# Feed-forward chunks for both images at once, the 64-channel remainders on halves of TensorE's array, and a new order of all pieces

## The chip, the cores and the metric

The kernel runs on one core of a Trainium2 chip. The metric is the device time in microseconds of one execution. A core has TensorE (PE, matrix products into PSUM), VectorE (DVE), ScalarE (ACT), GpSimd (POOL) and SyncE (SP, which here only issues DMAs). Each engine works through its own instructions in order; semaphores tie the engines together.

## The reference, cut to what matters

```python
h = tokenize(x)                       # 64 images, 196 patches of 768 values, layernorm, W: 768 -> 192, + positions
h = concatenate([h, txt], axis=1)     # 196 + 128 = 324 tokens of 192 channels per image
h = h + attn(layernorm(h))            # selective scan: h_t = exp(delta*A)*h + delta*B*x, y = sum over 16 states of h*C
h = h + ffn(layernorm(h))
# ffn: routed part: sigmoid gate over 128 experts, top 6, each expert silu(x@Wg)*(x@Wu)@Wd with hidden size 464
#      shared part: silu(x @ Wsg) * (x @ Wsu) @ Wsd with hidden size 928, for every token
```

All is float32. The change touches the shared part of `ffn`, and the order of everything that runs beside it.

## The kernel before

`build` runs two phases. `phase1` handles the images two at a time (32 pairs): embedding, first layernorm, the scan over 16 states, second layernorm, the gate and the choice of experts, and the shared feed-forward part. `phase2` goes through the 128 experts and adds their results to the output rows by indirect DMA. The change touches `phase1`, and of the preparation before it two memsets.

A tensor with 192 channels lies as three slabs of 324 columns: slab 0 holds channels 0 to 127 of image 0, slab 1 the same of image 1, and slab 2 holds the 64 remaining channels of both images, image 0 on partitions 0 to 63 and image 1 on partitions 64 to 127. A scan over one state is thus one instruction of 128 x 972.

**Pieces.** Phase 1 is software-pipelined. Its work for one pair is cut into pieces (`scan`, `up_g`, `down`, ...), each with a lag: body i of the loop runs a piece of lag 2 for pair i-2. `schedule` gives every piece a place between 0 and 32 for each engine it uses; the pieces sorted by place are the order of that engine's instructions, the same in every body. The places of different engines are tied to each other only by the semaphores. What sets the order is therefore this list, written out by hand: `scan` n at 2n, and the other pieces around it.

**The scan.** For state n: SP loads `b_wide` (piece `fill_b`, line 437) and `c_wide` (`load_c`, line 443), both broadcasts of a DRAM row to 128 partitions, each by two DMAs of 64 partitions; POOL multiplies `du` by `b_wide` into `state` (line 498); ACT writes the decay into PSUM (`decay`, lines 530 and 531); DVE scans (line 628) and multiplies by `c_wide` (`fill_c`, line 633); POOL adds into `y` (line 508). `b_wide`, `c_wide` and the decay are double-buffered, `state` has four buffers. Before that `bc_values` puts the rows in DRAM, `load_s` fetches one row from there, and `step_size` and `softplus` (ACT, lines 590 to 597, DVE, lines 703 to 705) make `delta` and `du`; line 705 is the last DVE instruction of it, once for each pair.

**The shared feed-forward.** The 928 hidden values are 8 chunks of 116. For chunk and image, 16 in all (k = 2 * chunk + image): `up_g` on PE is two matmuls (line 780 with the 128 channels, line 781 with the slab of remainders, against weights that are zero on the other image's 64 partitions), ACT takes tanh (line 607), DVE makes `ag` (line 765); `up_u` on PE is two matmuls again, and DVE makes `inter` (line 771). The two images use two PSUM banks and two buffers of `th` and `ag`, so one image's chunk can be on PE while the other's is on ACT or DVE. `down_a` and `down` (line 795) multiply `inter` by `ws_d` for each of three row blocks, 8 matmuls for each image and block, and DVE adds them to `h` (line 639).

**Others on PE.** `emb_a` and `emb` (lines 838 and 842): 12 matmuls each for one half image (6 of two columns for the sum of squares, 6 of 194 columns). `resid`, `x1_turn`, `x2_turn`, `gate`, `bc_values`, `count` are short and share one PSUM bank, `work`; `emb` and `down` share another, `sums`. `ln1_apply` and `ln2_apply` are 12 ACT instructions in a row (lines 564 and 565).

Of the kernel before, what the change touches and what calls it, by code (L numbers as in the profile page):

```python
# [9 lines left out]
ALU = mybir.AluOpType  # L10
# [8 lines left out]
PAIRS = B // 2  # L19
# [36 lines left out]

def schedule(engine):
    at = []  # L60

    def put(piece, lag, k, **steps):
        if engine in steps:
            at.append((steps[engine], len(at), (piece, lag, k)))

    for n in range(N):

        b, lag = 2 * n - 4, 0
        if b < 0:
            b, lag = b + 32, -1  # L70
        put("fill_b", lag, n, sp=b, pool=b + 3)
        c, lag = 2 * n - 2.3, 0
        if c < 0:
            c, lag = c + 32, -1
        put("load_c", lag, n, sp=c)
        d, lag = (2 * n - 1.5, 0) if n else (30.5, -1)
        put("decay", lag, n, act=d + 0.3)
        put("scan", 0, n, dve=2 * n)
        put("fill_c", 0, n, dve=2 * n + 1.2, pool=2 * n + 2)
    for k in range(3):  # L80
        put("down_a", 3, k, pe=0.1 + 2 * k)
        put("down", 3, k, pe=1.1 + 2 * k, dve=2.1 + 2 * k)
        put("store_out", 3, k, sp=3.6 + 2 * k)
        put("resid", 1, k, pe=4.9 + 1.8 * k, dve=5.7 + 1.8 * k)
        put("x2_turn", 1, k, pe=15.2 + 1.1 * k, act=16.2 + 1.1 * k)
        put("x1_turn", -1, k, pe=18.2 + 1.1 * k, act=19.2 + 1.1 * k)
    put("load_x", -2, 0, sp=1.5)
    put("load_txt", -1, 0, sp=10.2)
    put("ln2_stats", 1, 0, dve=10.3, act=11.3)
    put("ln2_apply", 1, 0, dve=12.3, act=13)  # L90
    put("emb_scale", -1, 0, dve=11.1)
    put("ln1_stats", -1, 0, dve=12.4, act=13.4)
    put("ln1_apply", -1, 0, dve=14.4, act=15.4)
    for k in range(2):
        put("gate", 1, k, pe=22.1 + k, act=23.3 + k)
        put("emb_a", -2, k, pe=8.5 + 6 * k, act=7.5 + 5.2 * k)
        put("emb", -2, k, pe=9.5 + 5.85 * k, act=13.2 + 5.85 * k)
    put("bc_values", -1, 0, pe=21.5, act=22.3, sp=22.9)
    put("load_s", -1, 0, sp=24.1)
    for k in range(2):  # L100
        put("step_size", -1, k, act=26.2 + k)
    put("softplus", -1, 0, act=28.5, dve=29.2)
    for k in range(3):
        put("choose", 2, k, dve=1.3 + k)
    put("weigh", 2, 0, dve=5)
    put("weigh", 2, 1, dve=6)
    put("count", 2, 0, pe=3.2, dve=5.2)
    put("store_mid", 2, 0, sp=6.5)
    put("find_a", 2, 0, dve=7.5)
    put("find", 2, 0, pe=7.6, dve=8.6)  # L110
    put("emb_stats", -2, 0, dve=20.4, act=21.4)
    for k in range(2 * NJ):
        for n, piece in enumerate(("up_g", "up_u")):
            step = 6.6 + 0.8 * (2 * (k // 2 * 2 + n) + k % 2)
            put(piece, 2, k, pe=step, act=step + 0.6, dve=step + 0.8)
    return [piece for _, _, piece in sorted(at)]
# [7 lines left out]
FIRST_BODY, LOOP_FROM, LOOP_TO, LAST_BODY = -2, 3, 29, PAIRS + 2  # L124
# [7 lines left out]
def bank_uses(i):  # L132

    return [sum(BANK.get(kind) == bank for kind, _, _ in pieces("pe", i)) for bank in (WORK, SUMS)]


def use_number(i, before):


    def use(piece, k, ago=0):  # L140
        bank = BANK[piece]
        same = [(x[0], x[2]) for x in pieces("pe", i - ago) if BANK.get(x[0]) == bank]
        return before[bank] - (len(same) if ago else 0) + same.index((piece, k)) + 1
    return use
# [35 lines left out]
class Buffers:  # L180


    def __init__(self, nc, ctx, ident, found):
# [18 lines left out]
        self.ws_g = sb("ws_g", [128, 3, SHID])  # L202
        self.ws_u = sb("ws_u", [128, 3, SHID])
# [36 lines left out]
def prepare(nc, ctx, a, out, dram_x, b):  # L240
# [4 lines left out]
    with ExitStack() as tmp:  # L245
# [9 lines left out]
        zero_tiles = [b.ident[:], b.ident_bf[:], b.wbc[:], b.wg[:, 1:3], b.ws_g[:, 1:3], b.ws_u[:, 1:3], b.zeros[:],  # L255
# [9 lines left out]
        for half in range(2):  # L265
# [4 lines left out]
                (b.wg[at, 1 + half, :], a["wg_t"][LO:D]), (b.ws_g[at, 1 + half, :], a["ws_g"][LO:D]),  # L270
                (b.ws_u[at, 1 + half, :], a["ws_u"][LO:D]),
# [92 lines left out]
def phase1(nc, ctx, a, out, dram_x, dram_cnt, dram_bc, ident, found):  # L364
# [54 lines left out]
    def bc_rows(t, half, first, rows):  # L419

        at = (2 * t.p + half) * N + first
        return dram_bc[at:at + rows]

    with nc.Block() as block:

        @block.sync
        def _(sp):
            def body(i, todo, use):
                for kind, lag, k in todo:
                    t = i.plus(-lag)  # L430
                    if kind == "fill_b":
# [7 lines left out]
                    elif kind == "load_c":  # L439

                        wait(sp, c_used, N * t.v + k - 1)
                        for half in range(2):
                            sp.dma_start(b.c_wide[k % 2][HI * half:HI * half + HI].rearrange("p a t -> p (a t)"),
                                         bc_rows(t, half, k, 1)[:, 3 * L:6 * L].broadcast_to([HI, 3 * L])).then_inc(c_loaded[k % 2], 16)
                    elif kind == "bc_values":

                        sp.wait_ge(work_free, use(kind, k))
                        wait(sp, c_used, N * (t.v - 1))
                        for image in range(2):
                            rows = b.bcv[N * image:N * image + N]  # L450
                            for half in range(2):
                                to = bc_rows(t, half, 0, N).rearrange("n (c q t) -> n c q t", c=3, q=3)
                                sp.dma_start(to[:, :, image, :], rows).then_inc(bc_stored, 16)
                                if half == image:
                                    sp.dma_start(to[:, :, 2, :], rows).then_inc(bc_stored, 16)
                    elif kind == "load_s":
# [3 lines left out]
                        for half in range(2):  # L460
                            sp.dma_start(b.soft[HI * half:HI * half + HI].rearrange("p a t -> p (a t)"),
# [679 lines left out]
```

## Time and profile before

| | us |
|---|---|
| median of 3 runs (lowest, highest) | 5815.71 (5800.55, 5816.44) |
| the profiled execution, its own time | 5808.81 |
| its span, first to last instruction | 5806.8 |
| PE, DVE busy | 4271.5 (74%), 3764.1 (65%) |
| POOL, ACT busy | 3097.6 (53%), 2051.7 (35%) |
| mean granted TensorE clock | 0.838 |

The span is cut into 40 slices of 145 us in part 2 of the page: phase 1 fills the first 28, phase 2 the rest. Busy shares over the whole span mix the two phases. The granted clock is 1.0 at 2.4 GHz and 0.5 at 1.2 GHz; a share between is a mix of both in time.

### The profile page before, as it was taken

What the parts mean: (1) busy time and instruction counts of PE and PEld (TensorE: products, weight loads), DVE (VectorE), ACT (ScalarE), POOL (GpSimd) and SP (SyncE); (2) the same over time, 40 slices, a digit from 0 to 9 for tenths busy, and PEclk for the clock granted to TensorE, in tenths of its full rate; (3) what the DMA queues carried; (4) which work ended last, traced back from release to release, by engine and by line L of the source; (5) the groups of instructions that cost most, each with busy time, mean ns of one, the idle gap of its engine ahead of it and who ended that gap; (6) DMA issues with size and microseconds to landing.
All of it is one profiled execution on the core that took longest, in us unless ns stands there. A gap on an engine that the chain in (4) does not pass through costs nothing. (4 is left out here: it accounts for less than half of the span.)

```text
span 5806.8 us, 71026 instructions
## 1 busy us (share of the span) xinstructions
PE 4271.5 (74%) x19964; PEld 3364.6 (58%) x19964; DVE 3764.1 (65%) x6446; ACT 2051.7 (35%) x3874; POOL 3097.6 (53%) x1769
## 2 busy tenths in 40 slices
PE   3357777777777777777777777777788788778877
PEld 2335555555555555555555555545677777777777
DVE  2778777778878778777777877786333333333333
ACT  2544454444445444454444445543111111111110
POOL 0765555555556555555555555653255555555554
PEclk7578878888878888878888888889888888888888
DMA  3776666666666666666666666663255555555554
GB/s 89 187 170 172 159 149 156 163 153 166 159 149 161 160 161 157 157 149 156 165 159 157 159 150 161 169 156 90 73 126 126 128 123 128 125 120 128 128 126 105
DMA packets 331418, 837.85 MB, mean 144 GB/s; under 512 B 59152, under 2 KB 143572, under 8 KB 331208
## 3 DMA queue, kind: packets, MB, share of 16 engines
q1 hardware_dynamic: 279928, 764.79, 52.7%
q0 software_dynamic: 49152, 69.84, 6.6%
q10 hardware_dynamic: 2128, 1.26, 0.1%
q14 instruction: 182, 1.49, 0.1%
q8 instruction: 28, 0.46, 0.0%
HBM read 761.92 MB, written 73.75 MB: 144 GB/s over the span
## 5 line engine op out<-in xcount | busy, mean ns | idle before, releaser
L508 POOL TENSOR_TENSOR y<-y,state 128x972 f32<-128x972 f32 x448 | 1027.8, 2294 | 1218.2 <-DVE state L633 1215.3
L498 POOL TENSOR_TENSOR state<-du,b_wide 128x972 f32<-128x972 f32 x512 | 1163.5, 2273 | 356.4 <-DMA b_wide<-bc_rows 191.8
L628 DVE TENSOR_TENSOR_SCAN ps<-ps,state 128x972 f32<-128x972 f32 x512 | 1117.8, 2183 | 106.6 <-POOL state L498 60.6
L780 PE MATMUL ps<-x2f,ws_u 128*116 128x324 f32 x1024 | 503.6, 581 | 574.3 <-DVE ag L765 572.8
L1053 PE MATMUL e_ps<-xgt,w_up 96*116 96x192 f32 x4096 | 730.5, 332 | 24.0 <-DVE e_ag L1026 23.9
L795 PE MATMUL ps<-ws_d,inter 116*98 116x192 f32 (+1 forms) x3072 | 604.9, 360 | 153.4 <-DVE h L639 134.1
L530 ACT ACTIVATE ps<-delta,a_neg 128x648 f32<-128x648 f32 x512 | 410.6, 802 | 855.9 <-DVE state L633 787.3
L1053 PEld LDWEIGHTS e_ps<-xgt,w_up 96*116 96x116 f32 x4096 | 677.3, 183 | 28.4 <-DVE e_ag L1026 26.7
L795 PEld LDWEIGHTS ps<-ws_d,inter 116*98 116x98 f32 (+1 forms) x3072 | 554.8, 193 | 207.6 <-DVE h L639 149.8
L780 PEld LDWEIGHTS ps<-x2f,ws_u 128*116 128x116 f32 x1024 | 190.5, 222 | 763.1 <-DVE ag L765 754.4
L633 DVE TENSOR_TENSOR state<-ps,c_wide 128x972 f32<-128x972 f32 x512 | 596.1, 1164 | 27.0 <-DVE ch L730 9.9
L1011 DVE TENSOR_TENSOR passed<-counts,tk 96x648 f32<-96x648 f32 x128 | 106.2, 829 | 760.9 <-DMA counts<-running_counts,row_idx 760.9
L964 POOL DMA_INDIRECT xg<-token_rows,gather_idx x256 | 244.9, 956 | 647.0 <-DVE gather_idx L1022 592.5
L765 DVE SCALAR_TENSOR_TENSOR ag<-th,ps 116x324 f32<-116x324 f32 x512 | 249.3, 488 | 443.7 <-ACT th L607 441.8
L607 ACT ACTIVATE th<-ps 116x324 f32<-116x324 f32 x512 | 217.2, 434 | 857.1 <-PE ps L781 857.0
L780 PE MATMUL ps<-x2f,ws_g 128*116 128x324 f32 x1024 | 424.2, 499 | 115.7 <-DVE inter L771 111.9
L1088 PE MATMUL e_ps<-w_down,e_inter 116*96 116x192 f32 x2048 | 495.6, 413 | 1.0 <-DVE e_inter L1038 1.0
L781 PE MATMUL ps<-x2f,ws_u 128*116 128x324 f32 x1024 | 455.5, 533 | 0.0
L1088 PEld LDWEIGHTS e_ps<-w_down,e_inter 116*96 116x96 f32 x2048 | 432.0, 217 | 32.7 <-DVE e_inter L1038 1.4
L973 POOL DMA_INDIRECT out_rows<-yo,scatter_idx x256 | 370.7, 1448 | 92.3 <-issue 78.0
L781 PE MATMUL ps<-x2f,ws_g 128*116 128x324 f32 x1024 | 391.7, 466 | 0.0
L842 PE MATMUL ps<-w_tok,x_in 128*98 128x194 f32 x1536 | 389.3, 420 | 0.0
(150 smaller groups left out, 6200.3 us busy)
## 6 DMA issues: line engine op xcount, KB each, us to landing
b_wide<-bc_rows SPq DMA_DIRECT2D x1024, 243.0 KB, 4.9
c_wide<-bc_rows SPq DMA_DIRECT2D x1024, 243.0 KB, 4.1
w_up<-in_we_up SPq DMA_DIRECT2D x128, 696.8 KB
w_down<-in_we_down SPq DMA_DIRECT2D x128, 348.0 KB
x_in<-in_x SPq DMA_DIRECT2D x32, 1176.0 KB, 8.0
soft<-bc_rows SPq DMA_DIRECT2D x64, 243.0 KB, 5.8
bc_rows<-bcv SPq DMA_DIRECT2D x192, 60.8 KB, 2.9
running_counts<-cnt SPq DMA_DIRECT2D x32, 324.0 KB, 3.8
```

Of the source, the lines that this page charges most:

```text
L498: nc.gpsimd.tensor_tensor(b.state[n % 4][:], b.du[t.p][:], b.b_wide[n % 2][:], ALU.mult).then_inc(input_ready, 1)
L508: nc.gpsimd.tensor_tensor(y, y, b.state[n % 4][:], ALU.add).then_inc(y_added, 1)
L530: nc.scalar.activation(to[:, 0:2 * L], b.delta[t.p][:, 0:2, :].rearrange("p a t -> p (a t)"), ACT.Exp, scale=b.a_neg[:, 0, k:k + 1])
L628: nc.vector.tensor_tensor_scan(s, s, b.state[k % 4][:].rearrange("p a t -> p (a t)"), 0.0, ALU.mult, ALU.add).then_inc(scan_done, 1)
L633: nc.vector.tensor_tensor(b.state[k % 4][:].rearrange("p a t -> p (a t)"), state_ps[k % 2], b.c_wide[k % 2][:].rearrange("p a t -> p (a t) ...
L780: nc.tensor.matmul(to, weights[:, 0, cols], b.x2f[t.p][:, q, :], start=True, stop=False)
L781: return nc.tensor.matmul(to, weights[:, 1 + q, cols], b.x2f[t.p][:, 2, :], start=False, stop=True)
L795: mm = nc.tensor.matmul(sums[0:ROWS[k], D * q:D * q + D], b.inter[:, j, q, OFF[k]:OFF[k] + ROWS[k]], b.ws_d[:, j, :], start=(j == 0), stop ...
L842: mm = nc.tensor.matmul(sums[0:98, 196 * c:196 * c + D + 2], b.x_in[:, k, f, at], b.w_tok[:, f, :], start=(f == 0), stop=(f == PC - 1))
L973: nc.gpsimd.indirect_dma_start(out, bass.IndirectOffsetOnAxis(ap=scatter_idx[t.p][:, q:q + 1], axis=0), yo[t.p][:, q, :], None, compute_op ...
L1053: mm = nc.tensor.matmul(ps[0:HC, to_bank + f // 2, CAP * (f % 2):CAP * (f % 2) + CAP], w_up[t.p][:, c, first + HC * f:first + HC * f + HC] ...
L1088: mm = nc.tensor.matmul(ps[0:HALF, 4, D * q:D * q + D], inter[:, f // 2, at:at + HALF], w_down[t.p][:, f, :], start=(f == 0), stop=(f == N ...
```

## The change

1. `up_g` and `up_u` take one chunk for both images: 8 pieces of each instead of 16. On PE a piece is four matmuls (two of 128 channels, two of 64). ACT and DVE get one instruction of 116 x 648 for two of 116 x 324. There is one buffer of `th` and of `ag`, and the two PSUM banks belong to one chunk, so `up_g` k+1 waits for `inter` k.
2. The remainders are multiplied from their own 64 partitions: image 0 with partitions 0 to 63 of weights and data, image 1 with 64 to 127. The zeroed halves of `ws_g` and `ws_u` and their memsets go.
3. `b_wide`, `c_wide` and `soft` are each loaded by one DMA of 128 partitions.
4. `down` and `emb` on PE are cut into four parts each, which can be placed apart (`down`: 4 matmuls each, 12 parts; `emb`: 6 matmuls each, 8 parts). The square of `x_in` on ACT is a piece of its own (`square`).
5. The hand-written places are replaced by a table `PLACES`; a place below 0 or above 32 gives the lag. Every engine's order changes. `load_x` has lag -3, so there is one more body at the start.
6. The count of uses of a PSUM bank is worked out from the order (`use`), with the same meaning.

```diff
+PLACES = {
+    "down": {
+        "pe": (91.23, 92.42, 92.43, 92.56, 94.43, 94.94, 95.9, 96.6, 97.04, 97.16, 97.4, 97.68,),
+        "dve": (102.09, 102.52, 104.48,),
+    },
...
+    "up_g": {
+        "pe": (61.71, 71.04, 73.41, 80.5, 84.48, 86.28, 86.98, 90.7,),
+        "act": (64.27, 70.8, 75.21, 77.26, 83.48, 85.06, 86.85, 92.25,),
+        "dve": (70.31, 75.21, 78.22, 84.67, 86.42, 89.59, 92.67, 96.24,),
+    },
+    "up_u": {
+        "pe": (66.38, 71.56, 79.79, 82.32, 84.85, 86.39, 90.39, 90.99,),
+        "act": (87.43, 98.17, 104.76, 107.65, 109.44, 112.61, 113.55, 125.49,),
+        "dve": (72.94, 76.49, 82.27, 85, 88.16, 91.16, 93.58, 97.56,),
+    },
...
-        self.ws_g = sb("ws_g", [128, 3, SHID])
-        self.ws_u = sb("ws_u", [128, 3, SHID])
+        self.ws_g = sb("ws_g", [128, 2, SHID])
+        self.ws_u = sb("ws_u", [128, 2, SHID])
...
-        zero_tiles = [b.ident[:], b.ident_bf[:], b.wbc[:], b.wg[:, 1:3], b.ws_g[:, 1:3], b.ws_u[:, 1:3], b.zeros[:],
+        zero_tiles = [b.ident[:], b.ident_bf[:], b.wbc[:], b.wg[:, 1:3], b.zeros[:],
...
-                        for half in range(2):
-                            sp.dma_start(b.b_wide[k % 2][HI * half:HI * half + HI].rearrange("p a t -> p (a t)"),
-                                         bc_rows(t, half, k, 1)[:, 0:3 * L].broadcast_to([HI, 3 * L])).then_inc(b_loaded[k % 2], 16)
+                        sp.dma_start(halves(b.b_wide[k % 2]), wide_row(t, k, 0)).then_inc(b_loaded[k % 2], 16)
...
-                        nc.scalar.activation(b.th[:, k % 2], gu_ps[:, k % 2], ACT.Tanh, scale=0.5).then_inc(th_ready, 1)
+                        nc.scalar.activation(b.th[:], gu_ps, ACT.Tanh, scale=0.5).then_inc(th_ready, 1)
...
-                        nc.vector.scalar_tensor_tensor(b.ag[:, k % 2], b.th[:, k % 2], 1.0, gu_ps[:, k % 2], ALU.add, ALU.mult).then_inc(g_used, 1)
+                        nc.vector.scalar_tensor_tensor(b.ag[:], b.th[:], 1.0, gu_ps, ALU.add, ALU.mult).then_inc(g_used, 1)
...
-                        nc.vector.tensor_tensor(b.inter[:, k // 2, k % 2], b.ag[:, k % 2], gu_ps[:, k % 2], ALU.mult).then_inc(inter_ready, 1)
+                        nc.vector.tensor_tensor(b.inter[:, k], b.ag[:], gu_ps, ALU.mult).then_inc(inter_ready, 1)
...
-                q, to, cols = k % 2, gu_ps[:, k % 2, :], slice(HC * (k // 2), HC * (k // 2) + HC)
-                nc.tensor.matmul(to, weights[:, 0, cols], b.x2f[t.p][:, q, :], start=True, stop=False)
-                return nc.tensor.matmul(to, weights[:, 1 + q, cols], b.x2f[t.p][:, 2, :], start=False, stop=True)
+                cols = slice(HC * k, HC * k + HC)
+                for q in range(2):
+                    nc.tensor.matmul(gu_ps[:, q, :], weights[:, 0, cols], b.x2f[t.p][:, q, :], start=True, stop=False)
+                for q in range(2):
+                    at = slice(HI * q, HI * q + HI)
+                    mm = nc.tensor.matmul(gu_ps[:, q, :], weights[at, 1, cols], b.x2f[t.p][at, 2, :], start=False, stop=True)
+                return mm
...
+                    if kind == "down":
+                        part, k = k % 4, k // 4
+                        if part == 0:
+                            pe.wait_ge(inter_ready, NJ * (t.v + 1))
+                        q, first = part // 2, NJ // 2 * (part % 2)
+                        for j in range(first, first + NJ // 2):
                             mm = nc.tensor.matmul(sums[0:ROWS[k], D * q:D * q + D], b.inter[:, j, q, OFF[k]:OFF[k] + ROWS[k]], b.ws_d[:, j, :],
                                                   start=(j == 0), stop=(j == NJ - 1))
-                        if q == 1:
+                        if part == 3:
                             mm.then_inc(sums_full, 1)
```

The orders that the table gives, from the start of a body (number of the piece behind its name, a prime for the next pair's scan, an asterisk where it is the last chunk of the pair whose other chunks ran in the body before):

```text
DVE: softplus, up_g7*, fill_c15*, scan0, up_u7*, choose2, weigh0, fill_c0, scan1, down0, count, up_g0, fill_c1, scan2,
     down1, weigh1, fill_c2, resid0, scan3, fill_c3, down2, scan4, resid1, fill_c4, up_u0, resid2, scan5, ln2_stats,
     emb_scale, up_g1, ln2_apply, fill_c5, up_u1, scan6, fill_c6, ln1_stats, up_g2, scan7, scan8, ln1_apply, fill_c7,
     up_u2, fill_c8, scan9, up_g3, fill_c9, scan10, up_u3, scan11, fill_c10, fill_c11, up_g4, scan12, up_u4, fill_c12,
     choose0, up_g5, choose1, up_u5, scan13, fill_c13, up_g6, scan14, up_u6, scan15, fill_c14, emb_stats
PE:  down7 to 11 with resid0 between, up_u0, resid1, resid2, emb0, emb1, emb2, up_g1, emb3, up_u1, emb4, up_g2,
     x2_turn0 to 2, emb5, gate0, emb6, up_u2, gate1, emb7, up_g3, x1_turn0, x1_turn1, up_u3, x1_turn2, bc_values,
     up_g4, up_u4, up_g5, up_u5, up_g6, up_u6, up_g7, up_u7, down0 to 3, count, up_g0, down4 to 6
ACT: decay1, up_g0, decay2 to 5, square0, decay6, square1, up_g1, ln2_stats, emb0, ln2_apply, decay7, x2_turn0, up_g2,
     x2_turn1, decay8, x2_turn2, ln1_stats, gate0, gate1, decay9, ln1_apply, up_g3, x1_turn0, decay10, x1_turn1,
     decay11, x1_turn2, bc_values, up_g4, decay12, decay13, up_g5, decay14, up_g6, emb1, decay15, step_size0,
     step_size1, softplus, up_g7, decay0', emb_stats
POOL: b3, c1, c2, b4, c3, b5, c4, b6, c5, b7, c6, b8, b9, b10, c7, b11, c8, c9, b12, c10, b13, b14, c11, b15, c12,
     c13, b0', c14, b1', b2', c15   (b is fill_b, c is fill_c)
```

## Rows read from the trace of the kernel before

**Rows 1.** The page, part 1: busy time, share of the span, instructions.
```profile
PE 4271.5 (74%) x19964; PEld 3364.6 (58%) x19964; DVE 3764.1 (65%) x6446; ACT 2051.7 (35%) x3874; POOL 3097.6 (53%) x1769
```

**Rows 2.** Windows: length, busy time of each engine, granted clock, DMA share, GB/s.
```profile
2000.00:3000.00 1000.00, 745.86 (x3075) 531.90 (x3075) 785.11 (x1221) 466.32 (x876) 565.43 (x251) 0.82 0.64 157
```

**Rows 3.** Line 705, all its instructions; then phase 2's first instruction in the timeline.
```profile
L705 DVE MEMSET delta<- x32: 61/61/61, 128.7 to 3887.3; 128x3 f32 x32
...
314.56 0.06 DVE L705 MEMSET delta<- 128x3 f32 x1
...
4129.64 0.13 POOL L913 IOTA slot_int<- 96x2 uint32 x1 [141.34 <-ACTq L909]
```

**Rows 4.** Waits of DVE from 1000 to 3000: us in total, times, longest.
```profile
DVE ag L765 <- ACT th L607: 224.5, 97, 5.8
DVE inter L771 <- PE ps L781: 114.7, 49, 5.8
DVE ps L628 <- POOL state L498: 22.2, 21, 4.1
```

**Rows 5.** Timeline of DVE: start, us, instruction, idle time before and its releaser.
```profile
2027.42 0.49 DVE L765 SCALAR_TENSOR_TENSOR ag<-th,ps 116x324 f32<-116x324 f32 x1 [5.13 <-ACT th L607]
...
2086.04 0.49 DVE L771 TENSOR_TENSOR inter<-ag,ps 116x324 f32<-116x324 f32 x1 [5.35 <-PE ps L781]
...
2108.94 0.49 DVE L765 SCALAR_TENSOR_TENSOR ag<-th,ps 116x324 f32<-116x324 f32 x1 [4.67 <-ACT th L607]
```

**Rows 6.** Timeline of ACT and PE around these three waits.
```profile
2025.18 0.93 ACT L590 ACTIVATE delta<-soft,bd,wd 128x648 f32<-128x648 f32 x1 [6.01 <-DMA soft<-bc_rows]
...
2080.46 4.18 PE L842 MATMUL ps<-w_tok,x_in 128*98 128x194 f32 x12
...
2112.23 0.44 ACT L564 ACTIVATE xm<-h,stat 128x64 f32<-128x64 f32 x1 [1.84 <-DVE stat L698]
...
2116.54 0.42 ACT L576 ACTIVATE x2f<-ps 128x324 f32<-128x324 f32 x1
```

**Rows 7.** Lines, forms apart, 1000 to 3000: busy us, mean ns, idle before.
```profile
L628 DVE TENSOR_TENSOR_SCAN ps<-ps,state 128x972 f32<-128x972 f32 x259 | 565.4, 2183 | 43.5 <-POOL state L498 22.2 <-issue 16.4 <-DVE ch L712 4.8
L633 DVE TENSOR_TENSOR state<-ps,c_wide 128x972 f32<-128x972 f32 x258 | 300.3, 1164 | 11.4 <-DVE ch L730 6.1 <-DVE top L717 3.6
L530 ACT ACTIVATE ps<-delta,a_neg 128x648 f32<-128x648 f32 x259 | 207.7, 802 | 434.3 <-DVE state L633 398.7 <-DVE delta L705 35.4
L765 DVE SCALAR_TENSOR_TENSOR ag<-th,ps 116x324 f32<-116x324 f32 x258 | 125.8, 488 | 225.7 <-ACT th L607 224.5
```

**Rows 8.** Timeline of PE: halves of a chunk at full clock, then at half clock.
```profile
2018.15 0.80 PE L780 MATMUL ps<-x2f,ws_u 128*116 128x324 f32 x2
...
2019.34 0.71 PE L780 MATMUL ps<-x2f,ws_g 128*116 128x324 f32 x2
...
2030.71 1.43 PE L780 MATMUL ps<-x2f,ws_u 128*116 128x324 f32 x2 [0.24 <-DVE ag L765]
...
2033.20 1.11 PE L780 MATMUL ps<-x2f,ws_g 128*116 128x324 f32 x2
```

**Rows 9.** Windows around them, columns as in rows 2.
```profile
2016.50:2021.50 5.00, 5.00 (x19) 2.86 (x17) 3.84 (x6) 2.03 (x5) 3.45 (x2) 1.00 0.93 218
2027.90:2033.20 5.30, 5.00 (x9) 2.19 (x9) 4.07 (x5) 5.24 (x8) 4.05 (x2) 0.50 0.53 128
```

**Rows 10.** Timeline of DVE in the last body, where only the feed-forward is left.
```profile
4100.53 0.49 DVE L765 SCALAR_TENSOR_TENSOR ag<-th,ps 116x324 f32<-116x324 f32 x1 [1.07 <-ACT th L607]
...
4105.12 0.49 DVE L765 SCALAR_TENSOR_TENSOR ag<-th,ps 116x324 f32<-116x324 f32 x1 [1.07 <-ACT th L607]
```

**Rows 11.** Timeline of DVE in the preparation.
```profile
2.02 1.60 DVE L317 MEMSET ws_g<- 128x1856 f32 x1 [0.33 <-issue]
...
5.55 0.22 DVE L317 MEMSET zeros<- 128x194 f32 x1
```

**Rows 12.** DMA issues: KB each, median us to landing.
```profile
b_wide<-bc_rows SPq DMA_DIRECT2D x1024, 243.0 KB, 4.9
```

More of the change, by code:

```diff
@@ L53, in wait @@
         eng.wait_ge(sem, value)
-def schedule(engine):
[L60 to L116, printed above, removed]
@@ L119 @@
+def schedule(engine):
+    at = [(places[k], name, k) for name, on in PLACES.items() for e, places in on.items() if e == engine for k in range(len(places))]
+    at = [(place % STEPS, -1 - i, (name, int(place // STEPS), k)) for i, (place, name, k) in enumerate(at)]
+    return [piece for _, _, piece in sorted(at, key=lambda x: (x[0], -x[1]))]
+STEPS = 32
 SCHEDULE = {engine: schedule(engine) for engine in ("pe", "act", "dve", "pool", "sp")}
+LAGS = [lag for pieces in SCHEDULE.values() for _, lag, _ in pieces]
@@ L123, with uses_bank, use @@
         "down": SUMS, "emb": SUMS}
-FIRST_BODY, LOOP_FROM, LOOP_TO, LAST_BODY = -2, 3, 29, PAIRS + 2
+LAST_PART = 3
+def uses_bank(piece, k):
+    return piece in BANK and (k % (LAST_PART + 1) == LAST_PART if BANK[piece] == SUMS else True)
+def use(piece, k, t):
+    mine = next((lag, at) for at, (p, lag, j) in enumerate(SCHEDULE["pe"]) if (p, j) == (piece, k))
+    total = 0
+    for at, (p, lag, j) in enumerate(SCHEDULE["pe"]):
+        if uses_bank(p, j) and BANK[p] == BANK[piece]:
+            first = PAIRS - 1 if p == "find" else 0
+            upto = t.v + (mine[0] - lag) + (0 if at <= mine[1] else -1)
+            if isinstance(upto, int):
+                total = total + max(0, min(upto, PAIRS - 1) - first + 1)
+            elif first == 0:
+                total = total + (upto + 1)
+    return total
 def pieces(engine, i):
     return [x for x in SCHEDULE[engine] if (PAIRS - 1 if x[0] in ("find_a", "find") else 0) <= i - x[1] < PAIRS]
[L132 to L144, printed above, removed]
 def run_bodies(eng, engine, body):
-    before = [0, 0]
-    add = lambda n, times: [b + x * times for b, x in zip(before, n)]
     for i in range(FIRST_BODY, LOOP_FROM):
-        body(Turn.fixed(i), pieces(engine, i), use_number(i, before))
-        before = add(bank_uses(i), 1)
-    steady = bank_uses(LOOP_FROM)
+        body(Turn.fixed(i), pieces(engine, i))
     with eng.Fori(0, (LOOP_TO - LOOP_FROM) // 2) as r:
@@ L157, in run_bodies @@
             start = Turn.fixed(LOOP_FROM + q)
-            so_far = [x + 2 * n * r for x, n in zip(add(steady, q), steady)]
-            body(Turn(start.v + 2 * r, start.p, start.h + r), pieces(engine, LOOP_FROM), use_number(LOOP_FROM, so_far))
-    before = add(steady, LOOP_TO - LOOP_FROM)
+            body(Turn(start.v + 2 * r, start.p, start.h + r), pieces(engine, LOOP_FROM))
     for i in range(LOOP_TO, LAST_BODY + 1):
-        body(Turn.fixed(i), pieces(engine, i), use_number(i, before))
-        before = add(bank_uses(i), 1)
+        body(Turn.fixed(i), pieces(engine, i))
 def build(nc, a, out):
@@ L417, in token_rows, with bc_rows, wide_row, halves @@
         return dram[bass.ds(t.v * (2 * L), 2 * L)].rearrange("(b r) d -> r b d", b=2)[OFF[k]:OFF[k] + ROWS[k]]
[L419 to L422 removed]
+    def bc_rows(t, half):
+        at = (2 * t.p + half) * N
+        return dram_bc[at:at + N].rearrange("n (c q t) -> n c q t", c=3, q=3)
+    def wide_row(t, n, c):
+        both = dram_bc[2 * t.p * N:2 * t.p * N + 2 * N].rearrange("(h n) (c f) -> n c h f", h=2, c=3)
+        return both[n, c].unsqueeze(1).broadcast_to([2, HI, 3 * L])
+    def halves(tile):
+        return tile[:].rearrange("p a t -> p (a t)")
     with nc.Block() as block:
@@ L459, in body @@
                         wait(sp, du_ready, t.v)
-                        for half in range(2):
-                            sp.dma_start(b.soft[HI * half:HI * half + HI].rearrange("p a t -> p (a t)"),
-                                         bc_rows(t, half, 0, 1)[:, 6 * L:9 * L].broadcast_to([HI, 3 * L])).then_inc(s_loaded, 16)
+                        sp.dma_start(halves(b.soft), wide_row(t, 0, 2)).then_inc(s_loaded, 16)
                     elif kind == "load_x":
```

229 lines of the change are left out of this document (172 added, 57 removed).

## The prediction

> **What bounds the kernel now.** I read the busy times first, then the windows, since the shares of the page mix two phases. In phase 1 no engine is full: from 2000 to 3000 us DVE is busy 79% of the time, PE 75%, POOL 57%, ACT 47% [rows 2], while the whole span has DVE at 65% [rows 1]. Phase 2 starts at 4129.6 us [rows 3] and its code is not touched, so 5806.8 - 4129.6 = 1677 us stay.
>
> The length of a body comes from the last DVE instruction of softplus, one for each pair: the third of the 32 is at 314.6, the last at 3887.3 [rows 3], so (3887.3 - 314.6) / 29 = 123.2 us. DVE's work in it is 0.785 x 123.2 = 96.7 us [rows 2]; it has the most, so a body can't be shorter than that, and 26.5 us of it are DVE's idle time. The waits say what it stands for: of 2000 us, 224.5 are `ag` waiting for ACT's tanh and 114.7 `inter` waiting for PE, together 339.2 x 123.2 / 2000 = 21 us for each body; waiting for POOL costs 1.4 us [rows 4]. The timeline shows that three waits of about 5 us make up 15 of it [rows 5]. The first stands behind ACT, which had waited 6.01 us for the DMA of `soft` with a tanh queued behind it; the second behind PE, which had an uninterrupted burst of `emb` ahead of `up_u` (its second half alone 4.18 us); the third behind ACT's rows of layernorm work [rows 6]. So phase 1 is bound by DVE's work plus the waits of an order in which ACT and PE have long things in front of short ones.
>
> **The change part by part.** I work with one body and multiply by 29; head and tail follow.
>
> *DVE's work.* 32 instructions of 324 columns become 16 of 648. One of 324 takes 0.49 us, one of 972 takes 1.16 us [rows 7], so one of 648 takes about 0.83. By durations that saves 16 x (2 x 0.49 - 0.83) = 2.4 us, but instructions one behind the other overlap at their ends, and what is saved could be near nothing. I take 1.0, so DVE's work is 95.7 us.
>
> *The long waits.* In the new order on ACT, `step_size` (behind the DMA) comes 10 pieces after `bc_values`, among them four decays that each wait for DVE: the load has over 20 us to land where 6 us were missing, so the first wait goes (-5.1). `emb` is in parts with `up_g1`, `up_u1`, `up_g2` between them, so at most 2 to 3 us of it stand in front of a chunk (the second wait, -5.4, goes but for that). The third stays in kind: ACT has gate1, decay9 and the twelve instructions of `ln1_apply` in front of `up_g3`. Twelve take 2116.54 - 2112.23 = 4.3 us [rows 6].
>
> *The hand-overs of a chunk.* Now there is one chunk in flight, and not two halves. From `ag` k to `inter` k PE must run four matmuls; from `inter` k to `ag` k+1 it must run four, and ACT a tanh of 648 columns. Two matmuls take 2019.34 - 2018.15 = 1.2 us at full clock (granted 1.00) and 2033.20 - 2030.71 = 2.5 us at half clock (granted 0.50) [rows 8, 9]; a chunk takes 2.3 or 4.9. ACT's 648 columns take 0.8 us [rows 7]. So DVE must have 2.3 us of other work between `ag` and `inter`, or 4.9 at half clock, and 3.1 or 5.7 between `inter` and the next `ag`. I go through DVE's new order with scan 2.2, `fill_c` 1.2 [rows 7] and the shorter pieces at 0.7 to 1.7:
> - `ag` to `inter`: chunk 0 is covered by a dozen pieces. Chunk 1 has ln2_apply and fill_c5 (1.8, wait 0.5 at full clock, 3.1 at half). Chunk 2 has 6 us, but the turns, emb5, gate0 and emb6 are in PE's queue ahead (0.5; 3.0). Chunks 3 and 7 have a scan and a fill_c, 3.3 (0; 1.6 each). Chunks 4 and 6 have one scan (0.1; 2.7 each). Chunk 5 has choose1, counted 1.2 (1.1; 3.7). Together 2.3 at full clock, 18.4 at half.
> - `inter` to the next `ag`: 0, 1, 6 and 7 are covered by 5 us and more. Chunk 2 to 3 has 3.3 us, and then ACT's queue as told above: 4.5 us, in both cases. Chunk 3 to 4 has 4.5 (0; 1.2), 4 to 5 has 2.9 (0.2; 2.8), 5 to 6 has 3.3 (0; 2.4). Together 4.7 and 10.9.
> - Others: `ln2_apply` for ACT's statistics 0.7, scan0 and scan4 for POOL 0.8 in all; 1.5.
>
> That makes 8.5 us of waits at full clock and 31 at half. The granted clock averages 0.82 now [rows 2], so PE is at half for (1 - 0.82) / 0.5 = 36% of the time. It falls where PE idles, and the two longest idle stretches of PE belong to the waits that go; but with one chunk in flight PE is idle for 1 to 3 us between any two of the late chunks. I take 25%: 8.5 + 0.25 x 22.5 = 14.1. **A body is 95.7 + 14.1 = 109.8, call it 110 us.**
>
> *The halves of the array.* No row shows a matmul of 64 partitions. A remainder matmul is half of 1.2 us; if image 0's and image 1's run at the same time each piece saves 0.6, 16 x 0.6 = 9.6 us of PE for each body, at worst it saves nothing and costs at each change of form as much as a start behind a wait does (0.80 against 0.71 us for the first pair of records [rows 8]), 32 x 0.1 = 3 us. On the path that is a share of the waits above, between -3 and +1 us for a body. I take 0: a float32 matmul shows two records [rows 8], the second on the same half as the first, so only the inner two of four can lie side by side.
> The Trainium skill speaks on both sides here. "TensorE: Matmul & The Clock Gate", Part 3, says that matmuls on different row groups run concurrently. "TensorEngine Tiling (Array Packing)", Tiling Modes, says that changing the tiling mode drains TensorE. By the first a body would be up to 3 us shorter than my sum, by the second up to 1 us longer; no run here shows either so far.
>
> *One DMA for two.* 486 KB instead of 2 x 243 KB that now fly together and land after 4.9 us [rows 12]. The DMA share is 0.64 at 157 GB/s [rows 2]; a body of 110 us needs 157 x 123.2 / 110 = 176 GB/s, or 0.72. Landing could take from 0 to 5 us longer; double buffering leaves some 7 us between two uses. I take nothing. SP's order has `load_c10` ahead of `fill_b12` and the like; those waits end before POOL needs the load, except for fill_b2', 1 us in POOL's slack.
>
> *POOL.* 565 / 1000 x 123.2 = 69.7 us of work for each body [rows 2], cover enough at 110 us.
>
> *Parts of `down`.* The same 96 matmuls; DVE has a scan, `count` or `weigh` between the three blocks. Nothing.
>
> *Head and tail.* Two memsets go from the start: 5.55 - (2.02 - 0.33) = 3.9 us [rows 11], ahead of every load, so all of it. The extra body holds only a load that started the kernel before too. In the last body only the feed-forward is left, and a chunk of both images takes 4105.12 - 4100.53 = 4.6 us [rows 10], as one half hides the other. Alone, a new chunk takes 2.3 + 0.8 + 0.8 + 2.3 + 0.8 = 7.0: 8 x 2.4 = 19 us longer, and half of that again in the body before, 30 us in all (90 at half clock, where it takes 12.2).
>
> **Sum.** Own time of the profiled execution 5808.8 (span 5806.8 and 2.0 around it), minus 29 x (123.2 - 110.0) = 383, minus 3.9, plus 30: 5452. The profiled execution is 6.9 us below the median of 5815.7, within the spread of the runs, so I say **5450**.
>
> **The rivals.**
> - *DVE's floor.* At full clock, and with the halves side by side, a body is 95.7 + 6 = 102: 5808.8 - 29 x 21.2 - 4 + 15 = 5205. For it: the new order keeps 2 to 6 us of DVE work in nearly each gap. Against it: the clock has to stay up through the gaps between the late chunks, where today's mean is 0.82 [rows 2].
> - *The waits come back.* If ACT or SP, whose orders are packed tighter, hold a chunk or a load in three more places by 3 us each, a body is 118: 5808.8 - 29 x 5.2 - 4 + 40 = 5694. For it: DVE waits for every engine in its order and each wait moves all behind it; all my waits are read in one pass with mean durations.
> - *PE's clock (the other side).* PE's work in a body is 0.746 x 123.2 = 92 us at a mean clock of 0.82 [rows 2], thus 76 us at full clock. One chunk in flight makes PE pause at each of 16 hand-overs. If that keeps it at half clock, all waits of the second column are paid, and PE has 76 / c us of work in the body, with some 20 us in which it can't but wait: at a mean clock c of 0.70 a body is 128 us, and 5808.8 + 29 x 4.8 - 4 + 85 = 6030. It decides from c = 76 / (123.2 - 20) = 0.74 downward. For it: the row of `up_u` at granted 0.50 came behind such idle time [rows 8, 9]. Against it: the mean is 0.82 with longer pauses than the new ones.
> - *The change doesn't do what it says*, the halves not side by side and the drains paid: within my sum at +1 us a body, 5480.
>
> **How the numbers follow.** Forecast (bodies of 105 to 115) 0.48, with 5310 to 5600 as its own range; floor 0.20; waits come back 0.17; clock 0.12; no effect at all 0.03. Below 5210 and above 5770 I leave less than 0.1 each, so the range is 5210 to 5770. Under 0.3% (17 us) a measurement can't tell from no change. Faster: 0.48 + 0.20 + 0.16 = 0.84; same 0.03; slower 0.13.
>
> **What would show it.** Line 705's counterpart every 110 us. DVE busy 87% of a steady window, with hand-over waits of some 12 us for each body, the longest of them before `ag` of chunk 3, behind `ln1_apply` on ACT. No wait of ACT for `soft`. Mean clock in phase 1 of 0.80 to 0.90. The four matmuls of a chunk in 2.0 to 2.3 us at full clock. The last body 20 us longer. I am wrong if PE's clock falls below 0.74, if DVE's waits for POOL or for `c_wide` come to more than 3 us, or if a new wait on SP appears.

## The result, and the profile after

The change makes the kernel slower: 12411 us (median) against 5809, a ratio of 2.135 (95% interval 2.129 to 2.141). The forecast was 5450, with a range of 5210 to 5770. The cause is the part that I had costed at nothing: the loads made by one DMA (e1 and e2 below show it).

Part 1 and the granted clock of the page of the changed kernel (part 1 is the counterpart of [rows 1]):

```profile
PE 4660.9 (38%) x19964; PEld 3434.9 (28%) x19964; DVE 3533.9 (29%) x5932; ACT 2069.2 (17%) x3618; POOL 3056.6 (25%) x1769
...
PEclk6555666656566556566665566666666655888888
```

The span more than doubled, and the work did not grow with it: DVE and POOL are busy for less than before, ACT for 17.5 us more, PE for 389 us more, with the same 19964 instructions at a mean granted clock of 0.644 where it had been 0.838. What grew is the waiting. A window of the steady part (the counterpart of [rows 2]), and the instruction that marks a body (of [rows 3]):

```profile
2000.00:3000.00 1000.00, 324.79 (x1166) 209.37 (x1166) 277.89 (x421) 178.44 (x306) 208.88 (x94) 0.60 0.16 60
...
L782 DVE MEMSET delta<- x32: 61/61/61, 130.5 to 10225.2; 128x3 f32 x32
```

From the first to the last of the 32 a body takes (10225.2 - 130.5) / 31 = 325.6 us on average; before it was (3887.3 - 128.7) / 31 = 121.2 [rows 3]. No engine is above 33%. The DMAs move 60 GB/s where they had moved 157 [rows 2], and their mean busy share is 0.16: of 16 DMA engines 0.16 x 16 = 2.6 are at work.

The waits of DVE and of POOL, 2000 to 3000 us (total, times, longest):

```profile
DVE state L710 <- DMA c_wide<-bc_rows: 502.6, 49, 24.7
DVE ps L705 <- POOL state L575: 162.4, 18, 11.2
...
POOL state L575 <- DMA b_wide<-bc_rows: 668.1, 49, 31.5
```

Each `fill_b` on POOL waits 668.1 / 49 = 13.6 us for `b_wide`, and each `fill_c` on DVE 502.6 / 49 = 10.3 us for `c_wide`. Before, from 1000 to 3000 us, the profile shows no wait of DVE for `c_wide`, and POOL waited for `b_wide` 62 times, 83.5 / 62 = 1.3 us at a time. The timeline of SP's DMA issues shows how fast the loads follow each other:

```profile
3212.62 9.33 SPq L523 DMA_DIRECT2D c_wide<-bc_rows  x1
3222.07 18.82 SPq L517 DMA_DIRECT2D b_wide<-bc_rows  x2
3240.94 18.82 SPq L523 DMA_DIRECT2D c_wide<-bc_rows  x2
3259.88 4.00 SPq L517 DMA_DIRECT2D b_wide<-bc_rows  x1
```

From the issue at 3212.6 to the one at 3259.9 there are five distances of 9.4 us each. An issue here takes as long as that itself, where before the two issues of a pair took 1.1 us together, so I read it as held back by the loads ahead. If two engines carry a load of 486 KB, each has 243 KB in 9.4 us, 26 GB/s (an estimate; the experiments show the two engines). A body has 33 such loads, 33 x 9.4 = 310 us of the 325.6 measured. The remaining 16 us I did not take apart; other transfers are slowed as well (`x_in` lands after 27.0 us in place of 8.0).

### The profile page after: what moved, and what is told of

The parts are those of the page before. It is cut to its first block and busy times, and to the rows that moved or that the text cites. A ratio compares the mean times of both kernels' runs of the same rounds, so it can differ in the third digit from the quotient of the medians.

```text
span 12367.0 us, 68150 instructions
## 1 busy us (share of the span) xinstructions
PE 4660.9 (38%) x19964; PEld 3434.9 (28%) x19964; DVE 3533.9 (29%) x5932; ACT 2069.2 (17%) x3618; POOL 3056.6 (25%) x1769
## 5 line engine op out<-in xcount | busy, mean ns | idle before, releaser
L858 PE MATMUL ps<-x2f,ws_u 128*116 128x324 f32 x1024 | 534.6, 666 | 2638.5 <-DVE ag L842 2638.5
L858 PEld LDWEIGHTS ps<-x2f,ws_u 128*116 128x116 f32 x1024 | 242.4, 261 | 2840.8 <-DVE ag L842 2749.7
L878 PE MATMUL ps<-ws_d,inter 116*98 116x192 f32 (+1 forms) x3072 | 711.4, 406 | 685.7 <-DVE inter L848 419.5
L858 PE MATMUL ps<-x2f,ws_g 128*116 128x324 f32 x1024 | 526.1, 657 | 1164.5 <-DVE inter L848 1164.5
L878 PEld LDWEIGHTS ps<-ws_d,inter 116*98 116x98 f32 (+1 forms) x3072 | 659.0, 227 | 760.9 <-DVE inter L848 388.8
L885 PE MATMUL ps<-ident,y 128*98 128x128 f32 (+1 forms) x288 | 83.8, 427 | 1526.3 <-DVE h L729 983.2
L858 PEld LDWEIGHTS ps<-x2f,ws_g 128*116 128x116 f32 x1024 | 243.9, 262 | 1377.0 <-DVE inter L848 1272.8
L885 PEld LDWEIGHTS ps<-ident,y 128*98 128x98 f32 (+1 forms) x288 | 44.2, 193 | 1568.2 <-DVE h L729 1013.1
L684 ACT ACTIVATE th<-ps 116x648 f32<-116x648 f32 x256 | 180.8, 706 | 1404.1 <-PE ps L861 1403.8
L936 PE MATMUL ps<-xf,wbc 128*96 128x324 f32 x192 | 112.0, 755 | 727.5 <-ACT xf L648 727.5
```

The source lines that it names most:

```text
L858: nc.tensor.matmul(gu_ps[:, q, :], weights[:, 0, cols], b.x2f[t.p][:, q, :], start=True, stop=False)
L878: mm = nc.tensor.matmul(sums[0:ROWS[k], D * q:D * q + D], b.inter[:, j, q, OFF[k]:OFF[k] + ROWS[k]], b.ws_d[:, j, :], start=(j == 0), stop ...
```

## The experiments

For each kernel the mean distance of a body is worked out as above, from the first to the last of the 32 instructions that end softplus. "Before" ran beside them at 5800 us (medians 5801.57, 5799.28 and 5800.1). The body is that of the one profiled execution: for e1 it was the shortest of its five (5375 us), for e6, e8 and e10 the longest (5579, 5544 and 5398). Small differences are therefore read from the medians and ratios, not from the bodies.

| kernel | median us | ratio to before (interval) | body, us |
|---|---|---|---|
| e1, two DMAs | 5428 | 0.937 (0.933 to 0.941) | 106.3 |
| e2, before with one DMA | 12429 | one run | 326.9 |
| e4, four engines | 7481 | one run | 172.1 |
| e7, eight engines | 5953 | one run | 123.8 |
| e3, full array | 5406 | 0.934 (0.929 to 0.938) | 106.8 |
| e5, old order | 6108 | 1.055 (1.051 to 1.058) | 130.1 |
| e6, uncut bursts | 5561 | 0.958 (0.954 to 0.962) | 113.0 |
| e8, ACT's order | 5523 | 0.951 (0.947 to 0.955) | 111.0 |
| e9, decays first | 5567 | 0.958 (0.955 to 0.962) | 113.0 |
| e10, decay9 first | 5366 | 0.925 (0.923 to 0.927) | 107.5 |
| e11, decay9 first, full array | **5283** | 0.910 (0.908 to 0.912) | 103.8 |

**e1: the DMAs undone.** `c` is 0, 1 and 2 for `b_wide`, `c_wide` and `soft`; the three waits count 32 again.

```diff
-                        sp.dma_start(halves(b.b_wide[k % 2]), wide_row(t, k, 0)).then_inc(b_loaded[k % 2], 16)
+    def load_halves(sp, tile, t, n, c, sem):
+        for half in range(2):
+            at = (2 * t.p + half) * N + n
+            sp.dma_start(tile[HI * half:HI * half + HI].rearrange("p a t -> p (a t)"),
+                         dram_bc[at:at + 1][:, 3 * L * c:3 * L * c + 3 * L].broadcast_to([HI, 3 * L])).then_inc(sem, 16)
```

> The changed kernel with one thing undone: b_wide, c_wide and soft are loaded by two DMAs of 64 partitions each again. Theory: a DMA whose source access begins with a dimension of 2 (the two halves) is spread over 2 DMA engines only, and that alone makes a body 325 us; with it undone a body is what the prediction worked out without it, 110 us (105 to 115), 5450 us in all (5310 to 5600). Rival: the new order or the chunk of both images holds the loads back; then it stays above 10000 us and POOL still waits for b_wide some 20 us at a time.

5428 us, 6.3% faster than before. The window and the marker of a body in e1:

```profile
2000.00:3000.00 1000.00, 746.05 (x3500) 497.41 (x3499) 839.25 (x1255) 538.02 (x932) 643.40 (x286) 0.85 0.73 181
...
L781 DVE MEMSET delta<- x32: 61/61/61, 123.9 to 3419.4; 128x3 f32 x32
```

The DMAs are back at 0.73 and 181 GB/s. Everything else in the change stands in e1, so undoing the loads alone takes the loss away. The theory's times held, and the rival fell.

**e2: only the DMAs, in the kernel before** (`halves` and `wide_row` of the change in place of the three pairs of DMAs, waits at 16).

> The kernel before, with the three loads made as the change makes them (one DMA of 128 partitions), and nothing else. Theory: the loads alone make the loss: some 33 loads a body at about 9.4 us each, a body of 310 to 330 us, about 11900 to 12500 us in all. Rival (order or chunks at fault): stays within 3% of 5810.

12429 us (one run), a body of 326.9 us: nearly that of the changed kernel (325.6), whose order is another and whose chunks are others. With e1 this shows from both sides that the loads are the cause; why a load is slow is the next pair's question.

**e4 and e7: the shape of the source alone.** The DMA of e1 with its 64 equal rows written as 4 x 16, and as 8 x 8:

```diff
-                         ....broadcast_to([HI, 3 * L])).then_inc(sem, 16)
+                         ....broadcast_to([4, 3 * L]).unsqueeze(1).broadcast_to([4, HI // 4, 3 * L])).then_inc(sem, 16)
```

> As e1 (two DMAs of 64 partitions), but each DMA's source is written with dimensions 4 x 16 x 972 in place of 64 x 972; bytes, rows and number of DMAs are the same. Theory (the first dimension of the source sets the number of DMA engines): 4 engines carry both, twice as many as in the changed kernel, so each load takes half as long, a body is about 165 us (155 to 180), 7000 us in all (6700 to 7500). Rival (what is slow is the size of one DMA, or reading two rows of DRAM in one): as fast as e1.

> As e1, but each of the two DMAs' sources written with dimensions 8 x 8 x 972: 8 DMA engines. A load of both halves should take about 486 KB / 8 engines, some 2.4 us where the row of four engines had 4.7. Theory: the loads of a body then take 33 x 2.4 = 80 us, under DVE's work: a body of 108 to 116 us, 5480 to 5750 us in all. Rival (loads must have all 16 engines for x_in and the stores beside them): above 5900.

Same bytes, same two DMAs, same rows of DRAM, and 7481 and 5953 us (one run each, far apart from e1's 5375 to 5447). Windows of e4 (2000 to 3000), then of e7:

```profile
2000.00:3000.00 1000.00, 562.36 (x2250) 374.87 (x2250) 512.24 (x789) 337.73 (x588) 397.35 (x179) 0.70 0.31 113
...
2000.00:3000.00 1000.00, 688.44 (x3111) 472.79 (x3112) 764.18 (x1112) 472.40 (x818) 561.03 (x252) 0.81 0.56 159
```

The DMA share goes 0.16, 0.31, 0.56, 0.73 with a first dimension of 2, 4, 8 and 64. Each is a little above 2, 4 and 8 of 16 (0.125, 0.25, 0.50), and a body goes 325.6, 172.1, 123.8, 106.3 us. The pages have a second count that fits exactly, the packets under 512 B in the whole execution (the changed kernel, then e1):

```profile
DMA packets 299662, 837.10 MB, mean 68 GB/s; under 512 B 27472, under 2 KB 111892, under 8 KB 299528
...
DMA packets 331344, 837.25 MB, mean 156 GB/s; under 512 B 59152, under 2 KB 143572, under 8 KB 331208
```

e4 has 33808 and e7 has 42256. e1, e7 and e4 make 32 x 33 x 2 = 2112 such loads and the changed kernel 1056. Take away 16, 8 and 4 small packets for each load in e1, e7 and e4, and 2 in the changed kernel, and the same 25360 are left in all four. So each load has as many small packets as the engines I count for it: 2, 4, 8 and 16. In these kernels the source's first dimension sets the number of engines; the destination's stayed at 64 (128 in the changed kernel).

For e4 the expectation held. For e7 it was too low: I had summed the loads (80 us) and left out that a load which takes longer also lands later than its reader wants it.

```profile
POOL state L574 <- DMA b_wide<-bc_rows: 533.6, 167, 9.1
...
DVE state L709 <- DMA c_wide<-bc_rows: 184.0, 76, 5.4
```

(e7, 1000 to 3000 us; in e1 these are 191.7 and 2.6.) The number of e7's rival (above 5900) came true; its reason, that `x_in` and the stores need all 16 engines beside the loads, was not tested.

The Trainium skill states a rule for the number of engines: "DMA: Bandwidth & Descriptors", Why a DMA increments its semaphore by 16 and not by 1, says that a copy runs on the largest k up to 16 that divides the slowest dimension (other than 1) of both source and destination. By that rule the change's 128 partitions against 2 x 64 rows give k = 2, and these four kernels agree with it.

**e3 and e11: the halves of the array undone** (three slabs of weights with zeros, full matmuls, same order), in e1 and in e10:

```diff
-                    mm = nc.tensor.matmul(gu_ps[:, q, :], weights[at, 1, cols], b.x2f[t.p][at, 2, :], start=False, stop=True)
+                    mm = nc.tensor.matmul(gu_ps[:, q, :], weights[:, 1 + q, cols], b.x2f[t.p][:, 2, :], start=False, stop=True)
```

> As e1, and the remainders are multiplied on the full array again, 128 partitions against weights padded with zeros, in the same place and order. Theory: halves of the array run only their inner two of four records side by side and PE is not what bounds: 0 to 3 us a body longer than e1, 0 to 90 us in all. Rival (a change of the tiling form drains PE, the Trainium skill's page TensorEngine Tiling): faster than e1 by up to 1 us a body, 30 us. Rival (all four side by side): PE busy falls by 9 us a body in e1 against this kernel.

A chunk on PE in e1 and then in e3, both at full clock:

```profile
2002.42 1.35 PE L857 MATMUL ps<-x2f,ws_u 128*116 128x324 f32 x4 [1.68 <-DVE ag L841]
2003.70 0.81 PE L860 MATMUL ps<-x2f,ws_u 64*116 64x324 f32 x4
...
2016.78 1.35 PE L857 MATMUL ps<-x2f,ws_u 128*116 128x324 f32 x4 [1.67 <-DVE ag L841]
2017.96 1.25 PE L859 MATMUL ps<-x2f,ws_u 128*116 128x324 f32 x4
```

The four records of the remainders take 0.81 us in place of 1.25: they do run side by side in part, and by more than the prediction's "only the inner two of four", which would leave 0.94. The first of them starts 1.28 us after the chunk's first in e1 and 1.18 in e3, so I put the change of form at 0.10 us (the next chunk in either kernel gives the same two distances). From start to end a chunk takes 2.09 us against 2.43, 16 x 0.34 = 5.4 us of PE for each body at full clock. And it buys nothing: 5428 and 5406 us, intervals overlapping. So "0 to 90 us longer" and the rival "up to 30 us faster" can't be told apart, and the rival of 9 us less PE in e1 fell. Windows 1000 to 3000 of e1, then of e3:

```profile
1000.00:3000.00 2000.00, 1503.26 (x7064) 1010.27 (x7062) 1676.18 (x2510) 1080.89 (x1885) 1291.71 (x576) 0.85 0.72 181
...
1000.00:3000.00 2000.00, 1524.32 (x7062) 1131.42 (x7061) 1669.74 (x2498) 1075.41 (x1884) 1292.01 (x573) 0.90 0.72 180
```

PE is busy for 1.4% longer on the full array (81.4 against 79.9 us for a body), but the granted clock is 0.90 and not 0.85.

> As e10, and the remainders on the full array, padded with zeros, as in e3. e3 had PE busy for 1.4% longer than e1 at a granted clock of 0.90 against 0.85, and the same time. Theory (what the halves save in records, the lower clock takes back): the same as e10 within 0.5%. Rival (the halves are worth their 4 us of PE a body where DVE waits less elsewhere): 1% slower than e10 or more.

Windows 1000 to 3000 of e10, then of e11:

```profile
1000.00:3000.00 2000.00, 1523.54 (x7089) 1029.33 (x7089) 1680.13 (x2508) 1081.28 (x1890) 1289.23 (x576) 0.84 0.72 181
...
1000.00:3000.00 2000.00, 1555.21 (x7324) 1164.21 (x7322) 1704.90 (x2593) 1114.98 (x1945) 1337.35 (x595) 0.91 0.75 187
```

Here the full array is even faster, 5283 against 5366 us (0.910 against 0.925, intervals apart), with the clock at 0.91 against 0.84. Theory and rival both said "same or slower" and both fell: in e10's order the halves of the array cost 1.6%. Both pairs show the halves together with a lower clock. That the clock is why e10 is slower is argued and not shown: of the 3.7 us between their bodies, `inter`'s waits for PE are 1.5 (85.4 and 60.5 us of 2000) and DVE's own busy time is 1.8.

**e5: the order undone, chunks of both images kept.** The new code with the hand-written places; chunk k at the mean place of its two halves.

> As e1 (two DMAs, chunks of both images, halves of the array), but with the hand-written places of the kernel before: chunk k of both images stands between the places of its two halves, and the parts of down and emb stand where the uncut pieces stood. Theory: the new order makes the gain of e1 (three long waits of DVE gone); with the old order ACT waits for soft again and emb stands before a chunk: a body of 119 to 126 us, 5700 to 5900 us in all. Rival (the chunks of both images make the gain, by fewer instructions and hand-overs): stays within 60 us of e1, about 5450.

6108 us, 5.5% slower than before and 680 us slower than e1. The long waits return:

```profile
DVE ag L779 <- ACT th L621: 258.8, 75, 6.9
DVE inter L785 <- PE ps L798: 184.2, 90, 5.0
...
ACT delta L604 <- DMA soft<-bc_rows: 101.0, 15, 7.8
```

(DVE, then ACT, 1000 to 3000.) DVE's hand-overs cost 443 us of 2000, against 339 before [rows 4] and 150 in e1; ACT waits 101.0 / 15 = 6.7 us for `soft` again. So the order makes the gain: with the other parts of the change in place, the old order is 5.5% slower than before and the new one 6.3% faster. The 5.5% belong to the chunk of both images with one buffer and the halves of the array taken together (the parts of `down` and `emb` stand at the old places here); the chunk was not tested alone, nor was the new order with the old chunks. The theory's range was 5700 to 5900 us, and the loss is 208 us beyond it.

**e6: bursts uncut.** `"pe": (91.23,) * 4 + (94.43,) * 4 + (97.04,) * 4` for `down`, `(-58.52,) * 4 + (-55.47,) * 4` for `emb`.

> As e1, with the four parts of each down and each half of emb placed together at the first part's place. Theory: the parts matter only where a chunk stands between them (emb behind up_u0 and up_u1, down 4 to 11 round resid and up_u0): 0 to 3 us a body longer than e1's 106 us, 0 to 90 us in all. Rival (the cut is what lets the order work): 5 us a body and more, over 150 us in all.

5561 us, 133 more than e1. `ag`'s waits for tanh rise from 89.3 to 162.2 us of 2000, the longest from 2.7 to 7.4 us; that one stands behind the four parts of half an `emb`, from 1263.8 to 1275.4 on PE, ahead of a chunk's `up_g`. By the medians that lies between my 0 to 90 us and the rival's 150. By the bodies the rival's "5 us a body and more" is met (113.0 against 106.3), but these are e6's longest and e1's shortest run, so neither is shown.

**e8, e9, e10: ACT's order.** `decay9` at 11.95 in place of 12.32 (ahead of `gate1`); in e8 and e9 also `up_g3` at 76.5 (ahead of `ln1_apply`), in e9 also `decay10` at 12.6.

> As e1, with two places on ACT changed: decay9 ahead of gate1, and up_g3 ahead of the twelve instructions of ln1_apply. In e1 DVE waits 1.3 us for decay9 and 2.7 us for chunk 3's tanh in each body. Theory: both waits go and nothing new comes but ln1_apply 2 us later, which has slack up to softplus: 2 to 4 us a body less, 60 to 110 us less than e1 in all. Rival: what is later now (x1_turn, bc_values, soft, softplus) ends at softplus, where DVE already waits, and gives it back: same as e1 within 20 us.

> As e8 (decay9 ahead of gate1, up_g3 ahead of ln1_apply), and decay10 ahead of ln1_apply too. Theory: e8 lost because decay10 stood behind the twelve instructions of ln1_apply, and DVE's scan10 waited 4.9 us for it; with decay10 ahead of them that wait goes and the two that e8 removed stay away: 2 to 4 us a body less than e1, about 5310 to 5370 us. Rival (the later ln1_apply itself costs, through x1_turn and up_u3 on PE): no better than e8, 5480 to 5540.

> As e1, with decay9 ahead of gate1 on ACT and nothing else. Theory: the 1.3 us for which scan9 waits on ACT in each body go, and ln1_apply and with it chunk 3's tanh come up to 1.3 us earlier: 1 to 2.5 us a body, 30 to 75 us less than e1 (5350 to 5400). Rival (the wait moves to the next piece): within 20 us of e1.

e8 is 95 us slower than e1, so its theory and its rival ("the same") both fell. Its timeline of DVE, and then that of e9:

```profile
2052.35 2.19 DVE L704 TENSOR_TENSOR_SCAN ps<-ps,state 128x972 f32<-128x972 f32 x1 [4.93 <-ACT ps L607]
...
2006.48 0.83 DVE L847 TENSOR_TENSOR inter<-ag,ps 116x648 f32<-116x648 f32 x1 [6.99 <-PE ps L860]
```

In e8 the wait moved to decay10, which stood behind the twelve instructions of `ln1_apply`; in e9 decay10 is ahead of them, and now `inter` 3 waits for PE, whose `up_u3` stands behind `x1_turn1`, which needs `ln1_apply`. The slack that I saw in `ln1_apply` was taken by PE's queue. e9's theory fell too; its rival was right that e9 is no better than e8, though 5567 us lies above its 5540. e10, the one step that makes nothing later, gains 1% (5366 against 5428, inside the 5350 to 5400 expected). e1's runs spread over 1.3%, but the intervals of the two ratios are apart. In e10's trace DVE's wait for that decay falls from 25.3 to 2.7 us of 2000, while `inter`'s waits for PE rise from 61.1 to 85.4: most of the wait moved, and where the 1% comes from the traces don't show.

## Why the prediction was wrong, by its steps

**The step that failed** is *One DMA for two*: "Landing could take from 0 to 5 us longer ... I take nothing." I had compared bytes (486 KB for 2 x 243 KB, 176 GB/s needed) and took for granted that one DMA is spread like two. It runs on 2 engines in place of 16: a body is 204 us longer than before (325.6 - 121.2), and against e1, where this step alone is undone, 325.6 - 106.3 = 219 us, where I had 0. The prediction's own sign of being wrong came with it: DVE's waits for `c_wide`, which were to stay under 3 us, are 0.5026 x 325.6 = 164 us for a body. None of my rivals was this one; the closest, "the waits come back", named a load held up, but priced it at 3 us. What could have warned me: `b_wide`'s DMA had 64 rows in source and destination, the new one has 128 rows against 2 x 64, and none of the rows I had read shows a load of that form. A part without a row needs a bound on both sides, as the halves of the array got one. The outer bound was at hand: 0.64 of 16 engines is the work of ten, and on fewer of them the loads could have been what limits the kernel.

**What held, read from e1, where only that step is undone.**
- The sum: 5452 forecast for it, 5428 measured (5310 to 5600 was its own range). The total is closer than its parts, and that is in part luck. In the profiled execution (span 5373.5) the distance of 31 bodies went from 3758.6 to 3295.5 us, 463 less, where I had 383; a body is 106.3 and not 110. The stretch from the last marker to phase 2 went from 242.3 to 294.3 us, 52 more, where I had 30; the first marker came 4.8 us earlier (3.9 from the memsets); phase 2, whose code is the same, took 17 us less. The median of the five runs is 53 us above this execution. Inside the body two errors work against each other: DVE works 6.5 us less than I had and idles 3.0 us more (17.1 against 14.1).
- DVE's work: 839.25 / 1000 x 106.3 = 89.2 us for a body, against my 95.7 and 96.7 before. The merged `ag` and `inter` gave the 2.4 us of the durations in full (15.5 us for a body before, 13.1 in e1). The rest is a term that I held fixed: the same instruction takes a different time at another place. Two of several, `du` in the kernel before and in e1, then `ch` in the same order (shortest/median/longest in ns):

```profile
L704 DVE TENSOR_TENSOR du<-delta,xf x32: 1170/3086/3101, 127.5 to 3884.1; 128x972 f32<-128x972 f32 x32
...
L780 DVE TENSOR_TENSOR du<-delta,xf x32: 1170/1170/1172, 122.7 to 3418.2; 128x972 f32<-128x972 f32 x32
...
L712 DVE TENSOR_TENSOR ch<-gt,e_bias x32: 957/958/959, 323.0 to 4053.2; 128x768 f32<-128x768 f32 x32
...
L788 DVE TENSOR_TENSOR ch<-gt,e_bias x32: 957/2870/3020, 286.4 to 3581.2; 128x768 f32<-128x768 f32 x32
```

Where I looked, the long ones lie beside a POOL instruction and the short ones in POOL's idle time: before, `du` at 2035.94 takes 3.09 us beside a `y` on POOL that takes 3.01 us itself (2.24 is its median), while the first `du`, at 127.47, takes 1.17 with POOL idle. The new order moved `du` out of POOL's way and `ch` into it. No run moves one of them alone, so this is read from the traces and not shown by an experiment.
- The three long waits: in e1 ACT has no wait for `soft`, and the longest hand-over wait, before `ag` of chunk 3, stands where I put it, behind `ln1_apply`, though it is 2.7 us and not 4.5:

```profile
2088.27 0.83 DVE L847 TENSOR_TENSOR inter<-ag,ps 116x648 f32<-116x648 f32 x1 [1.23 <-PE ps L860]
...
2091.49 2.19 DVE L704 TENSOR_TENSOR_SCAN ps<-ps,state 128x972 f32<-128x972 f32 x1 [1.30 <-ACT ps L607]
2096.39 0.83 DVE L841 SCALAR_TENSOR_TENSOR ag<-th,ps 116x648 f32<-116x648 f32 x1 [2.72 <-ACT th L683]
```

- The hand-overs: `ag` 89.3 and `inter` 61.1 us of 2000, together 150.4 / 2000 x 106.3 = 8.0 us for a body, where the list had 7.0 at full clock and about 12.6 at my quarter of half clock. What the list lacked or had too small is other waits: 40.6 us of 2000 before `delta`, for which the profile names no releaser, 43.3 of the scans for a decay or for POOL, 26.4 for ACT's statistics, together 5.9 us for a body. The clock is 0.85, so the rival of PE's clock had no part in the loss; the 0.60 of the changed kernel came with a PE that waited for the loads, and went with them.
- The halves of the array: "I take 0" held in time for e1, but beside two things that I hadn't in it, 5.4 us of PE saved at full clock and a lower granted clock; in e10's order they cost 1.6%.
- Parts of `down` and `emb`: I wrote "Nothing" for `down` alone; both together are worth 133 us (e6), which my walk had only in the second long wait.

## What to carry to other kernels

Before you merge DMAs, write down the first dimension of both sides as the instruction carries it, and ask among how many engines it can be divided: here 64 against 64 used all 16, and 128 against 2 x 64 used two, for the same bytes. In a profile the sign is a low DMA share together with engines that wait for loads; here 0.16 of 16 engines. An order can be forecast by reading its queues and hand-overs, but check the parts and not only the total, since here the total was within 1% with parts off by more; and ask of every DVE instruction that moves whether POOL will be working beside it. Test each part of a change by itself: this one held a gain of 6.3%, a loss of a factor of 2, and a part (the halves of the array) that is better left out; e11, with two DMAs, the full array and one decay moved, is at 0.910 of the kernel before.

## What the runs showed of the hardware that I had not expected

- With loads whose source begins with a dimension of 2, 4 or 8 the DMA share is 0.16, 0.31 and 0.56, and the counts of small packets fit 2, 4 and 8 engines exactly; one engine carries about 26 GB/s of these broadcasts (an estimate, 243 KB in 9.4 us).
- The same DVE instruction on the same tile, `du` of 128 x 972, took 1170 ns with POOL idle and 3086 ns (median) in the kernel before, where the one looked at ran beside a POOL instruction.
- Matmuls on the two halves of the array (64 partitions each, float32) take 0.81 us for four records against 1.25, and the change of form 0.10 us; with them the granted clock is 0.85 against 0.90, and 0.84 against 0.91.
